# One core, one fused block: a load moved ahead of two others on the sync queue, other warming products at the end, another DRAM layout for the convolution's input

## The chip, the core and the metric

The kernel runs on one core of a Trainium2 chip. The metric is the device time of one execution in microseconds. The core has a matrix engine (PE, with PEld its weight loads), a vector engine (DVE), a scalar engine (ACT), a general engine (POOL), and a sync engine (SP) that issues nearly all transfers. All transfers from SP go through one queue, q1, that 16 DMA engines serve.

## The reference

The input x has 128 samples of 32 channels by 512. Per sample, and with float32 results to match:

```
# 1: a 1x1 convolution whose weights are a softmax mix of 8 sets, chosen per sample by cond
agg_w = einsum('bk,koi->boi', att, weight); y = einsum('boi,bih->boh', agg_w, x) + agg_b
# 2: causal attention on y, 32 query heads, 8 key/value heads, head size 16, rope; residual
x = x + attention(y, Wq, Wk, Wv, Wo)
# 3: a grouped convolution along the 512, 9 taps, 4 groups, plus ctx(cond) and a bias
z = conv_general_dilated(x, weight, padding=[(4, 4)], feature_group_count=4) + ctx + bias
# 4: a linear layer and LoRA experts, weighted by the top 8 of 15 router probabilities; residual
x = x + z @ base_W.T + base_b + lora(z, top8(softmax(z @ router_W.T)))
```

## The kernel before

**Tiling.** The 128 samples are cut into 32 groups of four. A group is a tile of 128 rows (4 samples x 32 channels) by 512 columns. Each large product in reduced float32 (fp32r) is made of three: high by high, high by low, low by high.

**Stages.** Every engine runs a function `steps(t)`, for t from -1 to 33, with the middle in a hardware loop. Step t works on three groups at once: group t+1 gets its mixing and its queries, keys and values (`mix`, `queries`, `keys_values`); group t its scores, softmax, values and output projection (`scores`, `transpose_p`, `values`, `project`); group t-1 its convolution (`conv`); group t-2 the transposition of the convolution's output, the router, the experts and the linear layer (`transpose_z`, `feed_forward`, `transpose_hw`, `lora`). The order within a step is written out by hand, and engines wait for one another by semaphores. `peeled(t, n)` is true where the step is unrolled and t is n; `live(u)` where group u exists.

**The convolution's way.** The nine taps become three products over shifted copies. The sum after attention, `x1`, lies in SBUF with one column of padding on either side (`x1p`, 128 x 4 x 130). SP stores it to a scratch tensor `x1_dram` (L367) and, once that has landed, loads it back three times, shifted by 0, 1 and 2 columns, into 3 x 32 partitions of `xc` (L358); `conv` (L579) waits for the three.

**The sync queue.** SP issues in program order; a wait stops all that is behind it. Before its steps it loads group 0's and 1's x, the values of group 0 (`load_values`: a store of `vS` to DRAM, a wait for it, four loads into `vB`), `baseW` (1 MB), and it stores the mixing weights of groups 4 to 31 (448 KB, L345), waits for that store, and reads them back in their block form in four loads (L277) with pieces of 128 bytes, followed by the 1792 KB broadcast of the mixing biases (`mixb`, L348). These late weights are first used in step 3. Only then comes step 0, whose first issue is group 2's x (`xm`, L354). In a step the order is: x of group t+2, the three loads of `xc` for group t-1, the values of group t+1, the output of group t-2, the store of `x1p` of group t, and `xr`.

**The end.** In step 32 (`G`) no attention is left. PE has the linear layer, router and experts of group 30, then 28 products of 32 rows by 512 columns in bfloat16 whose result nobody reads (`keep_warm`, L433), then the convolution of group 31. Step 33 has the linear layer, router and experts of group 31.

Of the kernel before, what the change touches and what calls it, by code (L numbers as in the profile page):

```python
# [7 lines left out]
F32 = mybir.dt.float32  # L8
# [7 lines left out]
P = 128  # L16
# [53 lines left out]
def live(u):  # L70

    return not isinstance(u, int) or 0 <= u < G
# [13 lines left out]
def build(nc, x, cond, fside, cW0, cb0, cW1, cb1, cW2, cb2, cweight, cbias, Wq, Wk, Wv, Wo,  # L86
          convw, convc, baseW, baseb, routerW, routerb, loraA, loraB, emap, const, out):
    with ExitStack() as ctx:
# [3 lines left out]
        def sem(name):  # L92
            return ctx.enter_context(nc.semaphore(name))
# [102 lines left out]
        oT_lo = sb("oT_lo", [P, NQ, NB, S], F32R)  # L196
        x1p = sb("x1p", [P, PH, P + 2])
        x1 = x1p[:, :, 1:P + 1]
        xc = scratch[0:SHIFTS * S, 0:NB * PH * P].rearrange("p (q n) -> p q n", n=P)
        z_hi = sb("z_hi", [P, PH, P], F32R)  # L200
        z_lo = sb("z_lo", [P, PH, P], F32R)
        arS = sb("arS", [P, NAR])
# [13 lines left out]

        mixb_dram = nc.dram_tensor("mixb_dram", [B, S], F32, kind="Internal").ap()
        v_dram = nc.dram_tensor("v_dram", [P, P], F32, kind="Internal").ap()
        x1_dram = nc.dram_tensor("x1_dram", [NB * PH, CG * PH, P + 2], F32, kind="Internal").ap()
        mixw_dram = nc.dram_tensor("mixw_dram", [B, S, S], F32, kind="Internal").ap()  # L220

        bank = [ctx.enter_context(nc.psum_tensor(f"bank{i}", [P, 512], F32)) for i in range(0)]
# [39 lines left out]
        ar_ps, ar_sb, lg_sb, top_sb = sem("ar_ps"), sem("ar_sb"), sem("lg_sb"), sem("top_sb")  # L262
        ex_sb, top2_sb, rest_sb, sel_sb, selE_sb = sem("ex_sb"), sem("top2_sb"), sem("rest_sb"), sem("sel_sb"), sem("selE_sb")
        we_sb, hw_sb, hwT_ps, hwT_hi_sb, hwT_lo_sb = sem("we_sb"), sem("hw_sb"), sem("hwT_ps"), sem("hwT_hi_sb"), sem("hwT_lo_sb")
        ffn_ps, last_sb, out_sb = sem("ffn_ps"), sem("last_sb"), sem("out_sb")

        x_g = x.rearrange("(g b) s d -> g (b s) d", b=NB)
        out_g = out.rearrange("(g b) s d -> g (b s) d", b=NB)
# [26 lines left out]
        @block.sync  # L295
        def _(sp):

            sp.dma_start(condS[:, :], cond).then_inc(ld["cond"], 16)
            sp.dma_start(cst[:, :], const).then_inc(ld["const"], 16)
            sp.dma_start(cW0S[:, :], cW0).then_inc(ld["cW0"], 16)  # L300
            sp.dma_start(cb0S[:, :], cb0.rearrange("(p a) -> p a", a=1)).then_inc(ld["cb0"], 16)
            sp.dma_start(cbiasS[:, :], cbias).then_inc(ld["cbias"], 16)
            sp.dma_start(cvS[:, :], convw.rearrange("o i k -> o (i k)")).then_inc(ld["convw"], 16)
            sp.dma_start(ccS[:, :], convc).then_inc(ld["cc"], 16)
            sp.dma_start(fsideS[:, :], fside.rearrange("(a o) -> a o", a=1)).then_inc(ld["fside"], 16)
            sp.wait_ge(ld["cW1"], 16)
            sp.wait_ge(ld["cb1"], 16)
            sp.dma_start(xm[:, :], group(x_g, 0)).then_inc(xm_in, 16)
            for c in range(KC):
                sp.dma_start(rawq[:, c, :], Wq[c * P:(c + 1) * P, :]).then_inc(ld[f"wq{c}"], 16)  # L310
            sp.dma_start(rawkv[:, :, 0:P], Wk.rearrange("(c p) n -> p c n", p=P)).then_inc(ld["wkv"], 16)
            sp.dma_start(rawkv[:, :, P:2 * P], Wv.rearrange("(c p) n -> p c n", p=P)).then_inc(ld["wkv"], 16)
            for j in range(PH):
                sp.dma_start(rawB[:, j, :, :], loraB.rearrange("e (p j) r -> j p e r", j=PH)[j]).then_inc(ld["B"], 16)
            sp.dma_start(rawA, loraA.rearrange("e r l -> (e r) l")).then_inc(ld["A"], 16)
            sp.dma_start(rawR[0:NR, :], routerW).then_inc(ld["R"], 16)
            sp.wait_ge(aggb_sb, 1)
            sp.dma_start(mixb_dram, aggb[:, :]).then_inc(aggb_dram, 16)
            for k in range(NKV):
                sp.dma_start(rawo[HD * k:HD * (k + 1), :, :],  # L320
                             Wo.rearrange("(k g d) n -> k d g n", k=NKV, g=NQ)[k]).then_inc(ld["wo"], 16)

            mixb_row = mixb_dram.rearrange("b s -> (b s)")
            sp.wait_ge(y_ps, 1)
            sp.dma_start(xm[:, :], group(x_g, 1)).then_inc(xm_in, 16)
            sp.wait_ge(aggb_dram, 16)
            sp.dma_start(mixb[:, P:4 * P], mixb_row[P:4 * P].partition_broadcast(P)).then_inc(mixb_in, 16)

            def load_values(u):

                sp.wait_ge(vS_sb, u + 1)
                sp.dma_start(v_dram.rearrange("(m b) c -> b m c", b=NB), vS[:, :]).then_inc(v_out, 16)
                sp.wait_ge(v_out, 16 * (u + 1))
                for k in range(HK):
                    sp.dma_start(vB[S * k:S * (k + 1), :, :, HD * k:HD * (k + 1)].rearrange("m b h d -> m (b h) d"),
                                 v_dram.rearrange("(m b) (h k d) -> k m (b h) d", b=NB, h=2, d=HD)[k]).then_inc(vB_in, 16)

            sp.wait_ge(pads_sb, 1)
            load_values(0)
            sp.dma_start(xr[:, :], group(x_g, 0)).then_inc(xr_in, 16)  # L340
            sp.dma_start(rawbase, baseW.rearrange("(p j) l -> p j l", j=PH)).then_inc(ld["base"], 16)
            sp.wait_ge(mixw_zero, 1)
            sp.wait_ge(aggw_act, 1)
            sp.wait_ge(aggw_dve, 1)
            sp.dma_start(mixw_dram[4 * NB:B, :, :], aggS[4 * NB:B, :, :]).then_inc(mixw_out, 16)  # L345
            sp.wait_ge(mixw_out, 16)
            load_mixw(sp, 4, G, mixw_in)
            sp.dma_start(mixb[:, 4 * P:], mixb_row[4 * P:].partition_broadcast(P)).then_inc(mixb_in2, 16)  # L348

            def steps(t):  # L350

                if live(t + 2):
                    sp.wait_ge(y_ps, t + 2)
                    sp.dma_start(xm[:, :], group(x_g, t + 2)).then_inc(xm_in, 16)  # L354
                if live(t - 1):
                    sp.wait_ge(x1_out, 16 * t)
                    for s in range(SHIFTS):
                        sp.dma_start(xc[S * s:S * (s + 1), :, :],  # L358
                                     x1_dram[:, :, s:s + P].rearrange("q r n -> r q n")).then_inc(xc_in, 16)
                if live(t + 1):  # L360
                    load_values(t + 1)
                if live(t - 2):
                    sp.wait_ge(out_sb, t - 1)
                    sp.dma_start(group(out_g, t - 2), outS).then_inc(out_st, 16)
                if live(t):
                    sp.wait_ge(x1_sb, t + 1)
                    sp.dma_start(x1_dram.rearrange("q (i j) n -> (q i) j n", j=PH), x1p[:, :, :]).then_inc(x1_out, 16)  # L367
                if live(t) and live(t + 1):
                    sp.dma_start(xr[:, :], group(x_g, t + 1)).then_inc(xr_in, 16)

            for t in range(0, 4):
                steps(t)
            with sp.Fori(4, G - 2) as t:
                steps(t)
            for t in range(G - 2, G + 2):
                steps(t)
            sp.wait_ge(out_st, 16 * G)

        @block.tensor
        def _(pe):  # L380
# [49 lines left out]
            def keep_warm(products):  # L430

                for _ in range(products):
                    mm(ps[:, 0, :], query16[0:S, :], causal16[0:S, :], start=True, stop=True)  # L433

            def prepare_base(phases):

# [83 lines left out]
            def lora(u):  # L520

                pe.wait_ge(hwT_hi_sb, u + 1)
                pe.wait_ge(hwT_lo_sb, u + 1)
                for n, (a, b) in enumerate(((hwT_hi, lora_hi), (hwT_hi, lora_lo), (hwT_lo, lora_hi))):
                    mm(ps[:, 6, 0:BASE6], a[:, :], b[:, 0:BASE6], start=False, stop=(n == 2))  # L525
                    last = mm(ps[:, 2, 0:P], a[:, :], b[:, BASE6:D], start=(n == 0), stop=(n == 2))  # L526
                last.then_inc(ffn_ps, 1)

            def project(u):

# [90 lines left out]
            def steps(t):  # L621
# [3 lines left out]
                    pe.wait_ge(base_lo_sb, PH)  # L625
                if live(t - 2):
                    transpose_z(t - 2)
                if peeled(t, -1):
                    pe.wait_ge(mixw0_sb, 1)
                    pe.wait_ge(aggb_sb, 1)  # L630
# [28 lines left out]
                    transpose_p(t)  # L659
                if peeled(t, G - 1):  # L660
                    values(t)
                if live(t - 2):
                    transpose_hw(t - 2)
                if live(t) and not peeled(t, G - 1):
                    values(t)
                if peeled(t, G):
                    lora(t - 2)
                    keep_warm(28)
                if live(t - 1):
                    conv(t - 1)  # L670
                if peeled(t, 1):
                    prepare_base((2, 3))

# [213 lines left out]
        def _(dve):  # L887
# [213 lines left out]
            def output(t):  # L1101

                dve.wait_ge(ffn_ps, t - 1)

                wait(dve, out_st, 16 * (t - 2))
                out3 = outS.rearrange("p (n j) -> p j n", j=PH)
                v.tensor_tensor(out3[:, 0:3, :], ps[:, 6, 0:BASE6].rearrange("p (j n) -> p j n", j=3), x1b[:, 0:3, :], ALU.add)
                v.tensor_tensor(out3[:, 3, :], ps[:, 2, 0:P], x1b[:, 3, :], ALU.add).then_inc(out_sb, 1)  # L1108

            def steps(t):  # L1110
# [89 lines left out]
```

## Time and profile before

| | |
|---|---|
| median of 3 runs | 660.11 us (657.11 to 661.21) |
| the profiled execution | 660.98 us |
| its span on the core | 659.1 us |
| mean granted clock of PE | 0.974 of full |
| PE busy | 627.8 us, 95% |
| DVE, ACT, POOL busy | 476.9, 200.2, 224.5 us |
| chain that ended last | PE 88%, DVE 4%, DMA 4% |

The span is what the profiler saw on the core; the time of that execution is 1.9 us longer. The chain is the work that ended last, followed back from the end. Clock 1.00 is 2.4 GHz, 0.50 is 1.2 GHz.

### The profile page before, as it was taken

How to read it: one execution, taken by the hardware profiler on the slowest of the kernel's cores; microseconds unless marked ns; L12 is line 12 of the kernel's file. 1: busy time of each engine (PE TensorE's matmuls, PEld its weight loads, DVE VectorE, ACT ScalarE, POOL GpSimd, SP SyncE). 2: the span in 40 equal slices, each digit the busy share in tenths (PEclk: the TensorE clock that was granted, in tenths of full speed). 3: DMA queues.
4: the chain of work that ended last, by engine and by line, in shares of the span. 5: the costliest groups of instructions: out<-in, count | busy, mean ns of one | idle time of the engine just before them, and what ended most of it. 6: DMA issues, size and time to landing. Idle time of an engine off the chain costs nothing.

```text
span 659.1 us, 13009 instructions
## 1 busy us (share of the span) xinstructions
PE 627.8 (95%) x4375; PEld 512.9 (78%) x4375; DVE 476.9 (72%) x1169; ACT 200.2 (30%) x475; POOL 224.5 (34%) x181
## 2 busy tenths in 40 slices
PE   5967999999999999999999999999999999999785
PEld 3646888888888888888888888888888888887534
DVE  3555787777887777777788777777778777777612
ACT  4332333233333233323233323332323332332200
POOL 6341333323332333332333333333233333332200
PEclk9997999999999999999999999999999999999956
DMA  7675443544545544344444555434444455433410
GB/s 171 119 215 157 105 108 81 113 88 98 118 116 119 120 120 106 100 86 85 107 118 116 120 120 118 104 98 83 85 116 119 116 120 120 119 87 79 100 41 16
DMA packets 121300, 71.20 MB, mean 108 GB/s; under 512 B 48341, under 2 KB 103285, under 8 KB 121032
## 3 DMA queue, kind: packets, MB, share of 16 engines
q1 hardware_dynamic: 119808, 70.53, 45.7%
q10 hardware_dynamic: 1336, 0.24, 0.2%
q0 software_dynamic: 144, 0.28, 0.2%
q8 instruction: 7, 0.11, 0.1%
q14 instruction: 5, 0.04, 0.0%
HBM read 51.49 MB, written 19.53 MB: 108 GB/s over the span
## 4 chain that ended last, share of the span: by engine, by line
PE 88%; DVE 4%; DMA 4%; SPq 1%; ACT 1%; issue 1%; ACTq 0%; DVEq 0%
PE ps L389 32%; PE ps L559 9%; PE ps L553 8%; PE ps L612 6%; PE ps L571 5%; PE ps L579 5%; PE ps L489 4%; PE ps L525 4%; PE ps L600 4%; DMA mixw_dram<-scratch 2%; PE ps L587 2%; PE ps L543 2%; PE ps L433 2%; PE ps L567 2%; DMA xm<-x 1%; PE ps L526 1%
## 5 line engine op out<-in xcount | busy, mean ns | idle before, releaser
L869 POOL TENSOR_TENSOR qk<-network,t 128x640 f32<-128x640 f32 x31 | 48.2, 1555 | 171.1 <-DVE t L1046 171.1
L389 PE MATMUL ps<-wqkv_hi,y_hi 128*128 128x512 f32 (+1 forms) x256 | 87.5, 342 | 1.6 <-DVE raw L1065 1.5
L389 PE MATMUL ps<-wqkv_hi,y_lo 128*128 128x512 f32 (+1 forms) x256 | 87.3, 341 | 0.0
L389 PE MATMUL ps<-wqkv_lo,y_hi 128*128 128x512 f32 (+1 forms) x256 | 87.1, 340 | 0.0
L881 POOL TENSOR_TENSOR raw<-x1p,basebB 128x512 f32<-128x512 f32 x32 | 49.3, 1541 | 81.8 <-DVE x1p L1119 81.8
L1054 DVE TENSOR_TENSOR qk_t<-ps,cst 128x512 f32<-128x512 f32 x32 | 22.1, 692 | 58.5 <-PE ps L541 58.5
L694 ACT ACTIVATE qk_t<-ps 128x512 f32<-128x512 f32 x32 | 19.1, 597 | 141.5 <-PE ps L543 141.5
L694 ACT ACTIVATE raw<-ps 128x256 f32<-128x256 f32 (+1 forms) x96 | 40.2, 453 | 65.8 <-PE ps L600 64.1
L756 ACT ACTIVATE raw<-raw 128x512 f32<-128x512 f32 x64 | 40.4, 632 | 55.3 <-DVE raw L1065 55.3
L853 POOL TENSOR_TENSOR raw<-raw,rz 128x512 f32<-128x512 f32 x32 | 33.6, 1051 | 66.9 <-DVE rz L1075 66.9
L389 PEld LDWEIGHTS ps<-wqkv_hi,y_hi 128*128 128x128 f32 x256 | 48.7, 190 | 9.3 <-DVE raw L1065 1.9
L389 PE MATMUL ps<-wo_hi,oT_hi 128*128 128x512 f32 x128 | 52.6, 411 | 1.5 <-DVE oT_lo L892 1.5
L389 PEld LDWEIGHTS ps<-wqkv_lo,y_hi 128*128 128x128 f32 x256 | 48.7, 190 | 6.0
L389 PEld LDWEIGHTS ps<-wqkv_hi,y_lo 128*128 128x128 f32 x256 | 48.6, 190 | 5.9
L876 POOL TENSOR_TENSOR raw<-raw,zero 128x512 f32<-128x512 f32 x32 | 33.3, 1042 | 54.1 <-DVE raw L1108 54.1
L1063 DVE TENSOR_REDUCE mx<-ps 128x16 f32<-128x512 f32 x64 | 43.9, 686 | 10.7 <-PE ps L571 10.7
L389 PE MATMUL ps<-wo_hi,oT_lo 128*128 128x512 f32 x128 | 50.7, 396 | 0.0
L389 PE MATMUL ps<-wo_lo,oT_hi 128*128 128x512 f32 x128 | 50.5, 395 | 0.0
L861 POOL TENSOR_TENSOR y_lo<-ys,y_hi 128x512 fp32r<-128x512 f32 x31 | 40.0, 1290 | 17.5 <-ACT y_hi L694 17.5
L1065 DVE TENSOR_TENSOR raw<-ps,mx 128x512 f32<-128x512 f32 x64 | 44.3, 692 | 2.2
L559 PE MATMUL ps<-ffn_lo,z_hi 128*128 128x384 f32 x128 | 43.7, 342 | 0.0
L559 PE MATMUL ps<-ffn_hi,z_lo 128*128 128x384 f32 x128 | 43.5, 339 | 0.0
(180 smaller groups left out, 1488.8 us busy)
## 6 DMA issues: line engine op xcount, KB each, us to landing
scratch<-x_dram SPq DMA_DIRECT2D x96, 256.0 KB, 5.0
x_dram<-x1p SPq DMA_DIRECT2D x32, 260.0 KB, 2.2
xm<-x SPq DMA_DIRECT2D x32, 256.0 KB, 3.5
xr<-x SPq DMA_DIRECT2D x32, 256.0 KB, 2.7
out<-raw SPq DMA_DIRECT2D x32, 256.0 KB, 2.1
v_dram<-vS SPq DMA_DIRECT2D x32, 64.0 KB
vB<-v_dram SPq DMA_DIRECT2D x128, 16.0 KB, 2.1
mixb<-mixb_dram SPq DMA_DIRECT2D x1, 1792.0 KB, 8.2
```

What stands on the lines that cost most here:

```text
L389: last = mm(dst, a, b, start=(n == 0), stop=(n == 3 * len(left) - 1))
L553: last = mm(ps[:, 7, 0:P + NAR], a, b[:, BASE6:D + NAR], start=(n == 0), stop=(n == len(terms) - 1))
L559: mm(ps[:, 6, 0:BASE6], a, b[:, 0:BASE6], start=(n == 0), stop=False)
L612: last = mm(ps[P // 2 * h:P // 2 * (h + 1), 4, b * P:(b + 1) * P], vB[:, b, h, :], prT[:, 2 * b + h, :], start=True, stop=True)
L694: return nc.scalar.activation(dst, src, ACT.Copy)
L756: nc.scalar.activation(pr[:, D * h:D * (h + 1)], sx[:, D * h:D * (h + 1)], ACT.Exp, scale=HD ** -0.5).then_inc(p_sb, 1)
L853: nc.gpsimd.tensor_tensor(p3, p3, rz[:, 0:16].unsqueeze(2).broadcast_to([P, 16, S]), ALU.mult).then_inc(pn0_sb, 1)
L861: nc.gpsimd.tensor_tensor(y_lo[:, :], ys[:, :], y_hi[:, :].bitcast(F32), ALU.subtract).then_inc(y_lo_sb, 1)
L869: nc.gpsimd.tensor_tensor(qk[:, :], t1, t2[:, :], ALU.add).then_inc(qk_sb, 1)
L881: nc.gpsimd.tensor_tensor(x1c, x1, basebB[:, :].rearrange("p (n j) -> p j n", j=PH), ALU.add).then_inc(x1c_sb, 1)
L1063: v.tensor_reduce(m, s3, AX.X, ALU.max).then_inc(mx_sb, 1)
L1065: v.tensor_tensor(sx[:, D * h:D * h + D].rearrange("p (h m) -> p h m", m=S), s3, m.unsqueeze(2).broadcast_to([P, 16, S]), ALU.subtract).th ...
```

## The change

Four edits. **Sync queue:** the load of group 2's x now stands ahead of `baseW`; the wait for the mixing weights' store, their four loads and the `mixb` broadcast become a function `late_mixing`, called in step 0 behind group 1's values. **Warming products:** the 28 are gone; instead, full-row fp32r products of 128 x 512 (`wo_hi` by `wo_hi`) stand in runs of three or four: in step 32, four ahead of `transpose_hw`, three behind it, three behind `conv`; in step 33, three behind `transpose_z` and three behind `transpose_hw`. **Experts' product:** in every group the three products for the first 384 columns come first and signal by themselves; the three for the last 128 columns follow and signal `last_ps`, for which DVE's second addition waits. **Layout:** `x1_dram` is stored row by row of the convolution, so that each of the 32 rows is 16 x 130 contiguous numbers; the three loads take one run of 2078 numbers per partition, and `xc` has a row step of 130.

```
-        x1_dram = nc.dram_tensor("x1_dram", [NB * PH, CG * PH, P + 2], F32, kind="Internal").ap()
+        x1_dram = nc.dram_tensor("x1_dram", [CG * PH, NB * PH, P + 2], F32, kind="Internal").ap()
...
+            sp.wait_ge(y_ps, 2)
+            sp.dma_start(xm[:, :], group(x_g, 2)).then_inc(xm_in, 16)
             sp.dma_start(rawbase, baseW.rearrange("(p j) l -> p j l", j=PH)).then_inc(ld["base"], 16)
...
-            sp.wait_ge(mixw_out, 16)
-            load_mixw(sp, 4, G, mixw_in)
-            sp.dma_start(mixb[:, 4 * P:], mixb_row[4 * P:].partition_broadcast(P)).then_inc(mixb_in2, 16)
+
+            def late_mixing():
+
+                sp.wait_ge(mixw_out, 16)
+                load_mixw(sp, 4, G, mixw_in)
+                sp.dma_start(mixb[:, 4 * P:], mixb_row[4 * P:].partition_broadcast(P)).then_inc(mixb_in2, 16)
 
             def steps(t):
 
-                if live(t + 2):
+                if live(t + 2) and not peeled(t, 0):
...
                     for s in range(SHIFTS):
-                        sp.dma_start(xc[S * s:S * (s + 1), :, :],
-                                     x1_dram[:, :, s:s + P].rearrange("q r n -> r q n")).then_inc(xc_in, 16)
+                        sp.dma_start(xcF[S * s:S * (s + 1), 0:x1_row],
+                                     x1_dram.rearrange("r q n -> r (q n)")[:, s:s + x1_row]).then_inc(xc_in, 16)
                 if live(t + 1):
                     load_values(t + 1)
+                if peeled(t, 0):
+                    late_mixing()
...
-                    sp.dma_start(x1_dram.rearrange("q (i j) n -> (q i) j n", j=PH), x1p[:, :, :]).then_inc(x1_out, 16)
+                    sp.dma_start(x1_dram.rearrange("r q n -> q r n"), x1p[:, :, :]).then_inc(x1_out, 16)
...
-                    mm(ps[:, 0, :], query16[0:S, :], causal16[0:S, :], start=True, stop=True)
+                    mm(ps[:, 0, :], wo_hi[:, 0, 0:P], wo_hi[:, 1, :], start=True, stop=True)
...
-                for n, (a, b) in enumerate(((hwT_hi, lora_hi), (hwT_hi, lora_lo), (hwT_lo, lora_hi))):
-                    mm(ps[:, 6, 0:BASE6], a[:, :], b[:, 0:BASE6], start=False, stop=(n == 2))
+                terms = ((hwT_hi, lora_hi), (hwT_hi, lora_lo), (hwT_lo, lora_hi))
+                for n, (a, b) in enumerate(terms):
+                    last = mm(ps[:, 6, 0:BASE6], a[:, :], b[:, 0:BASE6], start=False, stop=(n == 2))
+                last.then_inc(ffn_ps, 1)
+                for n, (a, b) in enumerate(terms):
                     last = mm(ps[:, 2, 0:P], a[:, :], b[:, BASE6:D], start=(n == 0), stop=(n == 2))
-                last.then_inc(ffn_ps, 1)
+                last.then_inc(last_ps, 1)
...
+                if peeled(t, G + 1):
+                    keep_warm(3)
...
+                if peeled(t, G):
+                    pe.wait_ge(sx_sb, 2 * G)
+                    keep_warm(4)
                 if live(t - 2):
                     transpose_hw(t - 2)
...
+                if peeled(t, G) or peeled(t, G + 1):
+                    keep_warm(3)
                 if peeled(t, G):
                     lora(t - 2)
-                    keep_warm(28)
                 if live(t - 1):
                     conv(t - 1)
+                if peeled(t, G):
+                    keep_warm(3)
...
+                dve.wait_ge(last_ps, t - 1)
                 v.tensor_tensor(out3[:, 3, :], ps[:, 2, 0:P], x1b[:, 3, :], ALU.add).then_inc(out_sb, 1)
```

SP's issues from group 0's `xr` on, before; `scratch<-x_dram` are the loads of `xc`, `raw<-L_ffn_base_W` is `baseW`:

```order
L340 DMA xr<-x 128x512
L341 DMA raw<-L_ffn_base_W 128x2048
L345 DMA mixw_dram<-scratch 112x1024
L277 DMA mixw<-mixw_dram 32x28x32 x4
L348 DMA mixb<-mixb_dram 128x3584
L354 DMA xm<-x 128x512
L332 DMA v_dram<-vS 4x32x128
L335 DMA vB<-v_dram 32x8x16 x4
L367 DMA x_dram<-x1p 128x520
L369 DMA xr<-x 128x512
L354 DMA xm<-x 128x512
L358 DMA scratch<-x_dram 32x16x128 x3
```

The same stretch with the change (its line numbers are those of the new file):

```order
L342 DMA xr<-x 128x512
L344 DMA xm<-x 128x512
L345 DMA raw<-L_ffn_base_W 128x2048
L349 DMA mixw_dram<-scratch 112x1024
L334 DMA v_dram<-vS 4x32x128
L337 DMA vB<-v_dram 32x8x16 x4
L278 DMA mixw<-mixw_dram 32x28x32 x4
L355 DMA mixb<-mixb_dram 128x3584
L376 DMA x_dram<-x1p 16x32x130
L378 DMA xr<-x 128x512
L361 DMA xm<-x 128x512
L365 DMA scratch<-x_dram 32x2078 x3
```

Group 2's x and group 1's values moved ahead of the late weights; the store of group 0's `x1p` still stands behind them, now directly.

PE in step 32, from the experts' product of group 30 to the transposition of group 31, before:

```order
L619 MATMUL ps<-cst,hw 128x128
L525 MATMUL ps<-lora_hi,hwT_hi 128x384
L526 MATMUL ps<-lora_hi,hwT_hi 128x128
L525 MATMUL ps<-lora_lo,hwT_hi 128x384
L526 MATMUL ps<-lora_lo,hwT_hi 128x128
L525 MATMUL ps<-lora_hi,hwT_lo 128x384
L526 MATMUL ps<-lora_hi,hwT_lo 128x128
L433 MATMUL ps<-causal,query 128x512 x28
L579 MATMUL ps<-scratch,convW 32x512 x4
L587 MATMUL ps<-cst,raw 128x128 x4
```

With the change:

```order
L442 MATMUL ps<-wo_hi 128x512 x4
L631 MATMUL ps<-cst,hw 128x128
L442 MATMUL ps<-wo_hi 128x512 x3
L535 MATMUL ps<-lora_hi,hwT_hi 128x384
L535 MATMUL ps<-lora_lo,hwT_hi 128x384
L535 MATMUL ps<-lora_hi,hwT_lo 128x384
L538 MATMUL ps<-lora_hi,hwT_hi 128x128
L538 MATMUL ps<-lora_lo,hwT_hi 128x128
L538 MATMUL ps<-lora_hi,hwT_lo 128x128
L591 MATMUL ps<-scratch,convW 32x512 x4
L442 MATMUL ps<-wo_hi 128x512 x3
L599 MATMUL ps<-cst,raw 128x128 x4
```

The 28 between the experts' product and the convolution are gone; runs of three and four stand around the router's transposition (L619, now L631) and behind the convolution.

## Rows read from the trace of the kernel before

**Rows 1.** The page: PE's share of the span; one DMA issue, KB each, us to landing

```profile
PE 627.8 (95%) x4375; PEld 512.9 (78%) x4375; DVE 476.9 (72%) x1169; ACT 200.2 (30%) x475; POOL 224.5 (34%) x181
...
x_dram<-x1p SPq DMA_DIRECT2D x32, 260.0 KB, 2.2
```

**Rows 2.** PE's waits, 80 to 590 us: us in total, times, longest

```profile
PE ps L619 <- DVE hw L1033: 0.4, 1, 0.4
```

**Rows 3.** The chain of waits, 28 to 68 us: start us, us, what

```profile
28.34 2.52 DMA v_dram<-vS
...
45.18 8.09 DMA xm<-x
...
53.31 2.07 PE ps L489 x8
...
66.12 1.00 PE ps L579 x8
```

**Rows 4.** Timeline of SP's issues: start us, us, engine, line, out<-in

```profile
42.27 2.09 SPq L277 DMA_DIRECT2D mixw<-mixw_dram  x4
...
45.65 0.56 SPq L332 DMA_DIRECT2D v_dram<-vS  x1
53.43 2.51 SPq L335 DMA_DIRECT2D vB<-v_dram  x4
```

**Rows 5.** Timeline, 36 to 53 us: the last work ahead of the idle stretch

```profile
41.16 0.27 ACT L694 ACTIVATE vS<-ps 128x128 f32<-128x128 f32 x1
...
45.13 0.60 PE L543 MATMUL ps<-cst,qk 128*128 128x128 f32 x4
...
47.06 1.51 POOL L881 TENSOR_TENSOR raw<-x1p,basebB 128x512 f32<-128x512 f32 x1 [4.88 <-DVE x1p L1119]
```

**Rows 6.** Windows of 1 us: width, busy PE, PEld, DVE, ACT, POOL, clock, DMA, GB/s

```profile
48.00:49.00 1.00, 0.00 (x0) 0.00 (x0) 0.00 (x0) 0.00 (x0) 0.57 (x1) 0.73 1.06 444
...
58.00:59.00 1.00, 1.00 (x7) 1.00 (x8) 0.97 (x2) 0.00 (x0) 0.11 (x1) 0.65 0.52 188
...
627.00:628.00 1.00, 0.33 (x1) 0.14 (x1) 0.27 (x2) 0.28 (x1) 0.00 (x0) 1.00 1.12 199
628.00:629.00 1.00, 0.76 (x5) 0.79 (x5) 0.10 (x1) 0.00 (x0) 0.00 (x0) 0.86 0.19 30
```

**Rows 7.** The chain of waits, 622 to 657 us

```profile
622.13 1.75 PE ps L553 x12
...
628.24 0.41 PE ps L525
...
629.65 12.05 PE ps L433 x28
641.71 1.91 PE ps L579 x8
...
644.39 1.13 PE ps L587 x4
...
647.00 3.06 PE ps L553 x12
...
653.37 0.30 PE ps L619
...
654.44 0.41 PE ps L525
...
655.52 0.84 DVE raw L1107
```

**Rows 8.** Timeline of group 31's loads of `xc`, and the landing of the third (issued 624.26)

```profile
623.37 1.38 SPq L358 DMA_DIRECT2D scratch<-x_dram  x3
...
DMA to landing us min/median/max: 5.1/5.1/5.1
```

**Rows 9.** Timeline of a step in the loop: loads of `xc`, and the convolution

```profile
332.88 1.39 SPq L358 DMA_DIRECT2D scratch<-x_dram  x3
...
342.24 1.06 PE L579 MATMUL ps<-scratch,convW 96*32 96x512 f32 x8
```

More of the change, by code:

```diff
@@ L198, in build @@
         x1 = x1p[:, :, 1:P + 1]
-        xc = scratch[0:SHIFTS * S, 0:NB * PH * P].rearrange("p (q n) -> p q n", n=P)
+        xcF = scratch[0:SHIFTS * S, 0:NB * PH * (P + 2)]
+        xc = xcF.rearrange("p (q n) -> p q n", n=P + 2)[:, :, 0:P]
         z_hi = sb("z_hi", [P, PH, P], F32R)
@@ L264, in build @@
         we_sb, hw_sb, hwT_ps, hwT_hi_sb, hwT_lo_sb = sem("we_sb"), sem("hw_sb"), sem("hwT_ps"), sem("hwT_hi_sb"), sem("hwT_lo_sb")
-        ffn_ps, last_sb, out_sb = sem("ffn_ps"), sem("last_sb"), sem("out_sb")
+        ffn_ps, last_ps, last_sb, out_sb = sem("ffn_ps"), sem("last_ps"), sem("last_sb"), sem("out_sb")
         x_g = x.rearrange("(g b) s d -> g (b s) d", b=NB)
@@ L323, in _ @@
             mixb_row = mixb_dram.rearrange("b s -> (b s)")
+            x1_row = NB * PH * (P + 2) - 2
             sp.wait_ge(y_ps, 1)
```

## The prediction, written before the changed kernel was run

> **What bounds the kernel now.** I read the page first: PE is busy 95% of the span, the next engine 72% [rows 1]. Then PE's waits: in the 510 us between 80 and 590 there is one, of 0.4 us [rows 2]. So the loop is bound by PE's own products, and whatever this change saves lies before 80 or after 590. The chain of waits shows two places. At the start it runs through the landing of group 2's x: issued at 45.18, landed 8.09 us later; PE's last product before it ended at 45.73 (45.13 + 0.60), its next begins at 53.31: 7.6 us of idle PE [rows 3, 5]. At the end, 28 products that nobody reads hold 12.05 us of the chain [rows 7].
>
> The windows add the clock. It falls at 48.5 (0.73 in that slice), 2.7 us after PE went idle, and is back at 58.7 (0.65), 5.4 us after the work resumed; at the end it falls at about 628.7 (0.86), just ahead of the 28 products, which then run at 1.2 GHz and do not bring it back in 12 us [rows 6, 7]. The convolution takes 1.00 us at 2.4 GHz and 1.91 at 1.2 [rows 3, 7].
>
> **The sync queue.** The removed wait is worth 7.6 us and the half clock behind it up to half of 5.4, 2.7 us. From 53.31 to the convolution of group 0 at 66.12 there are 12.8 us; at full clock that stretch is 10.1 at least, and 10.6 if part of it was waiting for DVE. With x there in time it starts at 45.7, so PE is ready for that convolution at 56.3 (55.8 to 56.8), 9.8 us earlier. That is what the edit would give alone.
>
> What is late next is the convolution's input. The store of group 0's `x1p` stood behind the late weights before, and stands directly behind them now; but the late weights themselves start later, since group 1's values come first. Step by step on SP:
> - group 1's `vS` is there at 41.43 [rows 5]. Its store takes 2.5 us to land [rows 3], to 43.95; the 1.4 MB of `baseW` and mixing weights ahead of it, now with 256 KB of x more, may make it 44.4. I take 44.2.
> - the four `vB` loads take 2.5 us to issue [rows 4]: 46.7. The `mixw` loads start there; before it was 42.27 [rows 4], so everything late is 4.4 us later.
> - The queue delivers in order: group 1's values, a store of 64 KB issued at 45.65 right behind the `mixb` broadcast and x, did not land before 53.4, when the loads that wait for it start, 7.8 us instead of 2.5 [rows 4, 3]. Group 2's x, second behind the 2.2 MB, landed at 53.27, 11.0 us after the first `mixw` load [rows 3, 4]. The store of `x1p`, ready since 47.0 (POOL starts on it at 47.06 [rows 5]), now has that place: 46.7 + 11.0 = 57.7, plus the cost of its smaller pieces (below), 58.3.
> - the three loads of `xc`: from the first issue at 623.37 to the third landing at 624.26 + 5.1 = 629.37 are 6.0 us [rows 8]. Old form: 64.3. New form: 62.2 to 64.3; I take 63.4.
>
> So PE stands still from 56.3 to 63.4, 7.1 us, nearly as long as before. The convolution comes 2.7 us earlier than at 66.12, and the clock, which fell 2.7 us into the old gap, falls in this one too; before, it had been back for 7 us when the convolution came, now about 5.4 us of work at 1.2 GHz follow it, 2.7 us lost. **Sum: 0**, between 1.5 us gained and 1.5 lost, if the queue works as the rows show.
>
> **The layout.** The store of `x1p` goes from 128 pieces of 2080 bytes to 512 of 520. No row has such a store. Lower bound: as now, 2.2 us [rows 1]. Upper: the loads of `xc` move 512-byte pieces at 199 GB/s [rows 6], 1.3 us for 260 KB, where the store can't take under nothing: 3.5 us. I take 0.6 us more, nearer the bottom, since most of the 2.2 is not transfer. For the loads, pieces grow from 512 to 8312 bytes. Below: nothing gained. Above: the broadcast, pieces of 14336 bytes, moves 444 GB/s [rows 6], so 768 KB take 1.8 us instead of 3.9, 2.1 us gained. I take 0.9: the broadcast writes 128 partitions, each of these loads 32.
>
> In the loop neither matters: the loads are issued from 332.88 and there 6.0 us later, 338.9, the convolution starts at 342.24 [rows 8, 9]: 3.3 us of slack in each step.
>
> The Trainium skill (SBUF — State Buffer, "Door 1: The DMA port swizzle") speaks against the larger gain: 32 neighbouring partitions reach 8 of the 16 ports that a DMA writes through. With its 435 GB/s for all ports, 218 GB/s for 8 is an estimate of mine, and the loads would then gain 0.3 us whatever the piece: by this rule of the Trainium skill `xc` at the start lands at 64.0, by the broadcast's row at 62.2. The trace's 199 GB/s lies under that ceiling, which doesn't prove it.
>
> On the store, DMA: Bandwidth & Descriptors ("How a descriptor splits into AXI transactions") says that a piece which does not start on a multiple of 256 bytes fetches bytes that it does not use; 520-byte rows start so nearly always. No row shows that cost; it would sit inside the 3.5 us above.
>
> **The experts' product.** The same six products, as many columns and weight loads; the loop gets nothing. DVE's added wait is for products three behind those it waited for, and over before its first addition (0.84 us) is. At the very end DVE now starts after three products instead of six: before 1.08 us after their start (655.52 - 654.44 [rows 7]), now some 0.75, **0.3 gained**.
>
> **The end.** At full clock, step by step, by [rows 7] unless said:
> - the 28 products go: **12.05**.
> - four products ahead of `transpose_hw` lie in the wait for the router; three behind it in the wait for `hwT` (1.07 us from 653.37 to 654.44, less 0.3 for the transposition, against 0.7). One of the 28 takes 12.05 / 28 = 0.43 us at 1.2 GHz, half of it at 2.4; for the heavier type I allow 0.24. Nothing.
> - the experts' product of group 30, 1.41 us (628.24 to 629.65) with the clock falling in it, takes 1.08 as that of group 31: 0.3.
> - PE is ready for the convolution at 629.3. Its input landed at 629.37; 0.6 later for the store, 0.9 earlier for the loads: 0 to 0.7 of waiting, I take 0.2 lost.
> - the convolution 1.91 to 1.00: 0.9. The transpositions, 1.13 to 0.55: 0.6. The router's products, 3.06 to 1.75, as in the step before: 1.3. From there to `transpose_hw` the chain went through DVE and ACT, 3.3 us at either clock: nothing.
> - three products behind the convolution (0.7) fit under DVE's addition of the bias (0.77, from 643.62 to 644.39); three behind the transpositions under 1.5 us of waiting: nothing.
>
> Sum 12.05 + 0.3 + 0.3 - 0.2 + 0.9 + 0.6 + 1.3 = **15.3 us**.
>
> **Against the runs.** 660.98 of the profiled execution less 15.3 is 645.7; that execution is 0.9 above the median, so **644.8** by the runs.
>
> **The rivals.**
> 1. *The start gains too.* If the store of `x1p` overtakes the broadcast, it lands 2.8 us after its issue at some 49.7 (46.7 and 3 us for issuing five loads), and the three loads 5.1 to 6.0 us on, at about 58: a stall of some 1.7 us, too short for the clock to fall. Gain 66.1 - 58 = 8.1 us instead of 0, at most the 9.8 from above. Time 636.7, down to 635.0. Against it speaks the store of `vS`, which overtook nothing [rows 4]. In between lies a broadcast that is done sooner: each us off the stall is one us, and below 2.7 us of stall the clock's 2.7 come on top. Chance 0.15 for the full case, 0.07 for the cases between.
> 2. *The clock falls at the end all the same.* PE still waits for the router ahead of `transpose_hw`, and for the bias and the split of group 31. Then the 0.3, 0.9, 0.6 and 1.3 are not gained, and the three products behind the convolution take 1.3 us at 1.2 GHz, 0.5 beyond their cover: 3.6 us less, gain 11.7: 648.4. For it: the old clock fell without any idle stretch as long as at the start. Against: 13 full-row products, about 3.1 us, are added between the router of group 30 and the linear layer of group 31, and with the products of all rows the clock came back at 58.7, while 32-row ones did nothing for it. Chance 0.16.
> 3. *Slower: the layout breaks the loop.* Store, wait, loads, convolution follow each other in each step, with 3.3 us of slack. Should the store of 520-byte pieces take more than 2.2 + 3.3 = 5.5 us (with the loads as before), each us beyond costs about 30 us in all. To turn 15.3 gained into 6.6 lost it takes 22 us, 0.7 a step, a store of 6.2 us: nearly three times as long. The bound above is 3.5. Chance 0.02, and 0.01 that it eats the gain just to within 1%.
> 4. *The change does not do what it says*: the stall moves from the load to the convolution is my forecast itself for the first edit. That the 28 products were no cost, because `xc` was what PE waited for, is excluded: it landed at 629.4, when they began.
>
> **How the numbers follow.** Forecast (stall moved, clock kept) 0.57; the rivals 0.22, 0.16, 0.03; 0.02 for what I don't see. The forecast's own range is 643 to 646.5, from the 1.5 us of the start on either side. For 8 in 10 it reaches up to the second rival with a lost start, 649.5, and down through the cases between to 637. 1% is 6.6 us, about what a measurement of this kernel tells from no change: faster 0.96, the same 0.02, slower 0.02.
>
> **What the profile after would show.** Right: PE's wait for `xm` gone, one of 5 to 8 us for `scratch<-x_dram` in its place, ending at about 63.4; the clock at 0.50 behind it; `vB` of group 1 issued near 44, the `x1p` store landing near 58; no wait in the loop; clock 1.00 from 620 to the end; the last convolution about 12 us earlier; the end of PE's work about 1 us after the last `hwT`. Wrong: a convolution of group 0 before 60 (rival 1), a low clock after the last projection (rival 2), a wait for `x_dram` in the loop (rival 3).

## The result and the profile after

The changed kernel takes 651.78 us (651.24 to 653.86, 4 runs) against 660.66 (657.11 to 662.28, 4 runs) for the kernel before: a ratio of 0.9879, 95% interval 0.9832 to 0.9925. It is faster by 1.2%, where 2.3% was forecast; 651.8 lies above the range that ended at 649.5. The profiled execution took 651.24 us with a span of 649.3, 9.8 us less than before; 15.3 had been summed.

PE's waits of the changed kernel, whole span: us in total, times, longest.

```profile
PE ps L591 <- DMA scratch<-x_dram: 10.7, 3, 8.0
```

Neither this line nor one like it was among the waits before. The wait for group 2's x is gone, and the convolution (L591, before L579) waits three times for its input: 8.0 us at the start, 1.0 in step 31, 1.8 before the last one. The DMA issues show what has become slower behind the last two of them (for the first, see below); KB each and median us from issue to landing, the first line from before, the two others after:

```profile
scratch<-x_dram SPq DMA_DIRECT2D x96, 256.0 KB, 5.0
...
scratch<-x_dram SPq DMA_DIRECT2D x96, 259.8 KB, 4.3
x_dram<-x1p SPq DMA_DIRECT2D x32, 260.0 KB, 4.5
```

The store of `x1p` takes 4.5 us where it took 2.2 [rows 1]: 4.0 at the least in 32 groups, where it had been 3.7 at the most. One load of `xc` lands 0.7 us sooner in the median.

**The start.** SP's issues (start us, us), and then the chain of waits:

```profile
44.16 2.51 SPq L337 DMA_DIRECT2D vB<-v_dram  x4
46.71 2.42 SPq L278 DMA_DIRECT2D mixw<-mixw_dram  x4
```

```profile
50.00 9.04 DMA x_dram<-x1p
...
59.90 4.99 DMA scratch<-x_dram
...
64.93 1.93 PE ps L591 x8
66.86 1.91 PE ps L451 x8
68.78 3.92 PE ps L398 x12
```

The first late load is issued at 46.71 (forecast 46.7). The store behind the late weights lands at 59.04 (forecast 58.3), its loads at 64.89 (63.4). The first convolution starts 1.2 us earlier than before [rows 3], at 1.2 GHz, and the clock, which fell at 60.9, is back only at 71.1 (the columns are those of [rows 6]):

```profile
60.00:61.00 1.00, 0.00 (x0) 0.00 (x0) 0.00 (x0) 0.00 (x0) 0.00 (x0) 0.93 1.15 316
...
71.00:72.00 1.00, 1.00 (x5) 0.78 (x5) 0.00 (x0) 0.00 (x0) 0.00 (x0) 0.95 0.00 0
```

So the transposition of queries behind the first output projection starts at 72.70 instead of 71.09: the start loses 1.6 us.

**The end.** The chain of waits, from the store of group 30 on (L442 are the warming products, L599 the transpositions of the convolution's output, L565 the router's products, L631 is the transposition in `transpose_hw`):

```profile
607.48 4.43 DMA x_dram<-x1p
...
617.83 1.07 PE ps L591 x8
...
623.88 3.99 DMA x_dram<-x1p
...
628.70 4.88 DMA scratch<-x_dram
...
633.62 1.32 PE ps L591 x8
634.94 1.58 PE ps L442 x3
636.52 0.87 PE ps L599 x4
...
638.87 1.76 PE ps L565 x12
...
643.88 0.33 PE ps L631
...
645.80 0.83 DVE raw L1127
```

The 28 products are gone from it, and the store and the loads stand in their place. The last convolution starts 8.1 us earlier than at 641.71 [rows 7], and right then the clock falls once more, to come back at 637.7:

```profile
634.00:635.00 1.00, 1.00 (x9) 0.14 (x1) 0.01 (x1) 0.00 (x0) 0.00 (x0) 0.65 0.27 102
...
637.00:638.00 1.00, 1.00 (x5) 0.75 (x3) 0.00 (x0) 0.59 (x1) 0.00 (x0) 0.64 0.00 0
```

### The profile page after: what moved, and what is told of

It reads as the page before. It is cut to its first block, busy times and chain, and to the rows that moved or that the text cites. A ratio compares the mean times of both kernels' runs of the same rounds, so it can differ in the third digit from the quotient of the medians.

```text
span 649.3 us, 12985 instructions
## 1 busy us (share of the span) xinstructions
PE 616.8 (95%) x4363; PEld 508.9 (78%) x4363; DVE 474.8 (73%) x1169; ACT 200.3 (31%) x475; POOL 224.6 (35%) x181
## 4 chain that ended last, share of the span: by engine, by line
PE 88%; DMA 6%; DVE 3%; SPq 1%; ACT 1%; issue 1%; DVEq 0%
PE ps L398 34%; PE ps L571 9%; PE ps L565 8%; PE ps L624 6%; PE ps L591 5%; PE ps L583 5%; PE ps L498 4%; PE ps L612 4%; PE ps L535 3%; DMA x_dram<-x1p 3%; DMA scratch<-x_dram 2%; PE ps L599 2%; PE ps L555 2%; PE ps L579 1%; PE ps L538 1%
## 5 line engine op out<-in xcount | busy, mean ns | idle before, releaser
L591 PE MATMUL ps<-scratch,convW 96*32 96x512 f32 x256 | 35.3, 623 | 10.7 <-DMA scratch<-x_dram 10.7
```

What stands on the lines that cost most here:

```text
L591: last = mm(ps[S * g:S * (g + 1), 5, :], convW[:, g, :, :].rearrange("p j o -> p (j o)"), xc.rearrange("p (b g) n -> p g b n", g=S // CG)[ ...
```

## The experiments

Ratios are to the kernel before, with 95% intervals. The start of this kernel varies between executions: the wait for group 2's x, 7.6 us in the profile before, was 2.8, 4.4 and 4.8 us in three others whose start has the old order. Where the end is compared, I therefore count from the end of the last output projection. The end varies too: from there to the end of the span it is 38.9 us in the profile before, 37.8 with the new layout alone and 36.6 with the new order alone, all three with the 28 products. So differences between single profiles of the end carry an uncertainty of some 2 us, unless the waits and the clock in them explain the difference.

### The old layout in the changed kernel

```
-                        sp.dma_start(xcF[S * s:S * (s + 1), 0:x1_row],
-                                     x1_dram.rearrange("r q n -> r (q n)")[:, s:s + x1_row]).then_inc(xc_in, 16)
+                        sp.dma_start(xc[S * s:S * (s + 1), :, :],
+                                     x1_dram[:, :, s:s + P].rearrange("q r n -> r q n")).then_inc(xc_in, 16)
...
-                    sp.dma_start(x1_dram.rearrange("r q n -> q r n"), x1p[:, :, :]).then_inc(x1_out, 16)
+                    sp.dma_start(x1_dram.rearrange("q (i j) n -> (q i) j n", j=PH), x1p[:, :, :]).then_inc(x1_out, 16)
```

Expected: 

> The changed kernel with the old layout of x1_dram and of its three loads; the other three edits stay. Theory (the store in 520-byte pieces lands 1.9 us later, 4.0 to 4.4 us instead of 2.1, and this costs wherever the convolution waits for it): the store lands in about 2.2 us again, the first convolution starts near 63.4 instead of 64.9, the wait of 1.0 us in step 31 is gone, the wait of 1.8 us before the last convolution shrinks to 0.2 or less, and with it the clock stays at 1.00 to the end, which is worth 1.5 us more. Sum 1.5 + 1.0 + 1.6 + 1.5: some 646 us. Rival A (the clock falls at the end whatever the wait): the same without the last 1.5, some 647.7. Rival B (the store is slow for its place in the queue, not for its pieces): 651.8, no change.

Measured: 648.46 us, ratio 0.9827 (0.9788 to 0.9867), which overlaps the changed kernel's interval; the reading rests on the profile. The waits, the DMA issue and the chain of its profile:

```profile
PE ps L589 <- DMA scratch<-x_dram: 6.9, 1, 6.9
```

```profile
x_dram<-x1p SPq DMA_DIRECT2D x32, 260.0 KB, 2.2
```

```profile
66.38 1.94 PE ps L589 x8
...
631.57 1.06 PE ps L589 x8
632.64 0.90 PE ps L440 x3
633.53 0.59 PE ps L597 x4
```

The store takes 2.2 us again, the waits in step 31 and before the last convolution are gone, and with them the fall of the clock at the end: the convolution takes 1.06 us. The span is 3.2 us shorter than the changed kernel's although the first convolution starts 1.5 us later than there (66.38; group 1's values came a microsecond later). By places: 0.8 lost up to the transposition of queries at the start, 1.1 gained from there to the end of the last projection, 2.9 behind it, which is the wait and the clock. Rival B is out: the store was slow for its layout, not for its place. Rival A did not happen in this execution: without the wait the clock stayed. That it was 648.5 and not 646 is the start, which the old layout did not make any faster: the store landed 12.8 us after the first `mixw` load was issued, against 12.3 in the changed kernel, and the three loads took 5.7 us against 5.8.

### The new layout alone

The kernel before with the layout of the change and nothing else.

Expected: 

> The kernel before with the new layout alone. Theory: the store takes 4.0 to 4.5 us in every step, the three loads about 0.3 us less than before; the loop hides it, step 31 pays 1.0 us, the last convolution pays nothing since its input lands under the 28 products: 661 to 662 us. Rival (the layout is harmless and only the queue order shifted the stores): store 2.2 us, 660.7 us, no wait in step 31.

Measured: 660.79 us, ratio 1.0026 (0.9994 to 1.0057). Its DMA issue in the profile:

```profile
x_dram<-x1p SPq DMA_DIRECT2D x32, 260.0 KB, 4.4
```

The wait in step 31 is 0.5 us, another of 1.4 stands at the first convolution, and there is none in the loop or before the last. The 28 products and the loop hid the slow store; the layout shows its price only once the products are gone. It gained nothing either.

### The order on the sync queue alone

The kernel before with the first of the four edits and nothing else.

Expected: 

> The kernel before with the sync queue's order of the change alone. Theory (the stall moves from group 2's x to group 0's convolution, since the store of x1p stands behind the late weights): no wait for xm, a wait of about 7 us for scratch<-x_dram ending near 63.5, the clock low until some 69 us; 659.5 to 661.5 us, no change. Rival (the start gained and other things lost it): the first convolution before 60 us and 651 to 653 us.

Measured: 662.39 us, ratio 1.0034 (1.0011 to 1.0057): slower by 0.3%. PE's waits:

```profile
PE ps L586 <- DMA scratch<-x_dram: 9.2, 1, 9.2
```

The convolution of group 0 starts at 66.17 and runs for 1.94 us. The wait for x has become a wait for the convolution's input. The convolution starts as late as before (66.12), and now the work at 1.2 GHz follows it: the transposition of queries starts at 72.69 instead of 71.09. The rival, a start that gained, is out.

This profile also shows the 28 products from another side. They start at full clock, and the clock falls under them while PE is busy without a gap; the chain, and two windows:

```profile
630.90 10.16 PE ps L440 x28
```

```profile
632.00:633.00 1.00, 1.00 (x6) 0.40 (x5) 0.00 (x1) 0.00 (x0) 0.92 (x1) 0.91 0.11 43
633.00:634.00 1.00, 1.00 (x3) 0.29 (x2) 0.00 (x0) 0.00 (x0) 0.12 (x1) 0.50 0.58 219
```

### The late weights behind group 0's convolution input

In `late_weights_later` the layout is the old one, and the late weights are moved once more (against the changed kernel, without the lines of the layout):

```
                 if live(t - 1):
                     sp.wait_ge(x1_out, 16 * t)
+                    if peeled(t, 1):
+                        sp.wait_ge(mixw_out, 16)
                     for s in range(SHIFTS):
...
+                if peeled(t, 1):
+                    late_mixing()
                 if live(t + 1):
                     load_values(t + 1)
-                if peeled(t, 0):
-                    late_mixing()
```

Expected: 

> Old layout, and the late weights moved once more: in step 1, behind group 0's three loads of xc and ahead of group 2's values. Theory: the store of x1p is issued at 46.7 and lands at 49, xc near 55, the first convolution starts at 56.4 without a wait and the clock never falls: 9 to 10 us less than the run with the old layout, some 636.5 us. Rival (the late weights take the next transfer instead: values or x1p of group 1 are late in step 2): a wait of 2 to 5 us on vB or scratch<-x_dram between 65 and 85 us, 639 to 642 us.

Measured: 639.43 us (639.12 to 640.11), ratio 0.9686 (0.9648 to 0.9725). The timelines of PE and then SP:

```profile
58.86 1.06 PE L591 MATMUL ps<-scratch,convW 96*32 96x512 f32 x8
```

```profile
49.10 0.33 SPq L376 DMA_DIRECT2D x_dram<-x1p  x1
...
51.14 1.52 SPq L365 DMA_DIRECT2D scratch<-x_dram  x3
52.71 6.01 SPq L277 DMA_DIRECT2D mixw<-mixw_dram  x4
```

The store is issued and landed within 2 us, and the first convolution starts without a wait, 7.5 us earlier than in the run with the old layout and at full clock. PE's waits have one more, of 1.0 us, for the convolution's input in step 2: the rival's wait, but smaller than its 2 to 5 us. It is 9.0 us less than in `old_layout`, where 9 to 10 were expected; the time itself lies 2.9 above the expected 636.5 and in the rival's range, since `old_layout` had come out at 648.5 and since here too group 1's values came late, so that the store was issued at 49.1 and not at 46.7. This is the fastest kernel of the study by its ratio.

### The same pair with the new layout

Expected: 

> The late weights in step 1 as in late_weights_later, with the new layout of x1_dram. The pair differs by the layout alone. Theory: the store lands in 4.0 to 4.5 us instead of 2.2; a wait of about 1 us in step 31, one of 1 to 2 us before the last convolution, 0 to 1 us before the first: 642 to 643.5 us against 639.4. Rival (the longer store is hidden once the queue is free): 639.4, as the pair's other kernel.

Measured: 646.5 us (643.2 to 649.37), ratio 0.9800 (0.9763 to 0.9836), against 0.9686 with the old layout. PE's waits in its profile, 40 to 80, 80 to 590 and from 590 us:

```profile
PE ps L593 <- DMA scratch<-x_dram: 2.2, 1, 2.2
...
PE ps L593 <- DMA scratch<-x_dram: 0.7, 1, 0.7
...
PE ps L593 <- DMA scratch<-x_dram: 2.3, 2, 1.6
```

Its span is 3.9 us longer than the old layout's (641.3 against 637.4), and the waits are the theory's: 2.2 us of the difference lie ahead of the end of the last projection, 1.7 behind it. The intervals of the two ratios do not overlap, so here the price of the layout shows in the times as well. At the end PE waits 1.6 us for the last convolution's input and the clock stays at 1.00; at the start it falls, at 59.0, and the first convolution takes 1.93 us. The profiled execution was the fastest of four that spread over 6 us; what the other three lost on top, no trace shows.

### What makes the store slow

Rows of 192 or of 144 numbers in `x1_dram`, same store, loads in pieces of 512 bytes:

```
-        x1_dram = nc.dram_tensor("x1_dram", [CG * PH, NB * PH, P + 2], F32, kind="Internal").ap()
+        x1_dram = nc.dram_tensor("x1_dram", [CG * PH, NB * PH, 192], F32, kind="Internal").ap()
...
+                    sp.dma_start(x1_dram[:, :, 0:P + 2].rearrange("r q n -> q r n"), x1p[:, :, :]).then_inc(x1_out, 16)
```

Expected, 768 bytes: 

> The changed kernel with rows of 192 numbers (768 bytes) in x1_dram: the store still moves 512 pieces of 520 bytes, now each from a multiple of 256 bytes; the three loads take pieces of 512 bytes. If the pieces' starts (and that neighbours share a line of DRAM) make the store slow, it lands in 2.2 to 2.8 us; if their number does, in 4.0 to 4.5 us as in the changed kernel. Only the store's time is read from this run; the loads should take about what they did before the change, 5.0 us.

Expected, 576 bytes: 

> The same with rows of 144 numbers (576 bytes): pieces start on multiples of 64 bytes, mostly not of 256. If only a shared line of 64 bytes is slow, the store lands in 2.2 to 2.8 us; if the start has to be a multiple of 256 bytes, it stays above 3 us where pitch768's is below; if the number of pieces is the cause, 4.0 to 4.5 us like pitch768.

Measured, the DMA issues of the two, in this order:

```profile
x_dram<-x1p SPq DMA_DIRECT2D x32, 260.0 KB, 3.4
```

```profile
x_dram<-x1p SPq DMA_DIRECT2D x32, 260.0 KB, 3.6
```

Neither theory alone. Of the 2.3 us between 2.2 and 4.5, pieces that start on a grid and no longer adjoin each other give 0.9 (576) to 1.1 (768) back. Most of it comes back already with starts on multiples of 64 bytes, of which one in four is a multiple of 256; whether the starts or the gaps between the pieces do it, these two runs can't tell. 1.2 us remain with 512 pieces in place of 128, each on its own row. Whether their number or their order in DRAM costs that was not told apart. The times, one run each (648.48 and 655.28), aren't compared.

The two say something of the clock as well. In both PE waits 1.8 us for the last convolution's input, as in the changed kernel. The chains of 768 and then of 576:

```profile
632.09 1.07 PE ps L591 x8
```

```profile
636.66 1.93 PE ps L591 x8
```

At 768 the clock stays at 1.00 to the end of PE's work; at 576 it falls at 636.6. So the same wait doesn't always bring the fall.

### No 28 products, and 28 of all rows

In the kernel before, the call of 28 products is taken out (`no_28`), or its product replaced (`full_row_28`):

```
-                    mm(ps[:, 0, :], query16[0:S, :], causal16[0:S, :], start=True, stop=True)
+                    mm(ps[:, 0, :], wo_hi[:, 0, 0:P], wo_hi[:, 1, :], start=True, stop=True)
```

Expected, none: 

> The kernel before without the 28 warming products and with nothing in their place. Theory (all of their 12 us lay on the path, since xc had landed): 12 us less, less up to 0.5 for xc, 648.5 to 649.5 us, with the clock low over the last convolution. Rival (part of their time covered the load of xc or the output of group 30): 651 to 654 us.

Measured: 647.56 us, ratio 0.9796 (0.9767 to 0.9825). Its chain:

```profile
622.70 5.21 DMA scratch<-x_dram
627.95 1.98 PE ps L579 x8
```

From the last projection to the end of the span 26.8 us remain of 38.9: 12.1 us, all of the products' time in the profile before. Against the two other profiles with the 28 products it is 11.0 and 9.8 us; there the products took 11.35 and 10.16 us, since the clock fell 0.7 and 1.9 us behind their start and not 0.9 ahead of it. This removal alone is faster than the whole change (its interval lies just below that of 0.9832 to 0.9925). The time of 647.56 lies 1 us below the 648.5 to 649.5 that were expected.

Expected, all rows: 

> The kernel before, its 28 warming products replaced by 28 full-row ones of 128 x 512 in reduced float32, at the same place. Theory (products of 32 rows do not bring the clock back, full-row ones do): the clock is back 3 to 7 us after the 28 begin, they take some 9 us instead of 12, and the last convolution runs at 2.4 GHz: about 3 + 0.9 + 0.6 + 1.3 = 6 us less than before, some 654.5 us. Rival (rows make no difference): 12 us of products, clock 0.50 until 652, about 660.5 us.

Measured: 654.17 us, ratio 0.9892 (0.9871 to 0.9913). Chain and window:

```profile
627.86 7.37 PE ps L433 x28
635.23 1.04 PE ps L579 x8
```

```profile
629.00:630.00 1.00, 1.00 (x4) 0.81 (x3) 0.00 (x0) 0.00 (x0) 0.94 (x1) 0.66 0.12 47
```

The clock is back at 629.7, 1.8 us after the products begin, sooner than the expected 3 to 7; in 12 us of 32-row products it did not come back [rows 7], nor in the two other profiles that have them. So the kind of the products decides. That it is the rows, as the theory said, isn't shown: the full-row products are reduced float32 where the 32-row ones are bfloat16, and no run changes one without the other. From the last projection to the end of the span 32.5 us remain of 38.9, 6.4 less (expected 6), and 7.4 us are still products that nobody needs. The clock did not stay either: it falls again at 639.9, in the router's products, which take 2.47 us.

### No warming products in the fastest kernel

Expected: 

> late_weights_later without any warming product. Theory (the short full-row products keep the clock at 2.4 GHz over the end): without them it falls between the last projection and the end, the last convolution takes up to 1.9 us instead of 1.0, the transpositions 1.1 instead of 0.6, the router's products up to 3.0 instead of 1.8: 641 to 643 us. Rival (nothing but the 28 products was the cost, and the clock would have stayed): 639.0 to 639.4, clock 1.00 throughout.

Measured: 641.83 us (638.03 to 642.17), ratio 0.9698 (0.9662 to 0.9734); the interval overlaps that of the kernel with them, so the times don't decide. In the profile the clock falls at 628.3; the window, and then the chain:

```profile
628.00:629.00 1.00, 0.88 (x5) 0.91 (x6) 0.00 (x0) 0.00 (x0) 0.00 (x0) 0.67 0.00 0
```

```profile
624.15 1.04 PE ps L591 x8
...
628.12 2.89 PE ps L565 x12
```

From the last projection to the end of the span it is 24.6 us, against 23.5 with the products, whose router products take 1.77: the 16 products are worth 1.1 us in these two executions. Another of the four executions without them took 638.03 us at a mean clock of 0.997, less than any with them (639.12 at least). No trace shows its end; its mean clock suggests that the fall does not come in every execution. What the products are worth on the average stays open.

## Why the prediction was wrong

**The step that failed** is the term of the layout, "I take 0.6 us more, nearer the bottom, since most of the 2.2 is not transfer". The store takes 2.3 us more in the median, 1.9 at the end (2.06 to 3.99), beyond the upper bound of 1.3. The bound was taken from loads of 512-byte pieces; that their rate also holds for stores of such pieces was not in any row, and neither was it that most of the 2.2 is not transfer. For the loads I took 0.9 of gain. At the end, where it counted, they gained 0.3: 5.7 us from the first issue to the last landing against 6.0. (Over all 32 groups the median of that stretch falls from 6.5 us to some 5.7, but in the loop nobody waits for it.) Behind this term hang three others:

- *Step 31.* The 3.3 us of slack were worked out for the loop, and with the end's 6.0 us for the loads; in the step of [rows 9] itself the third load lands 6.6 us after the first issue, which leaves 2.7. That was still enough. Step 31 has no next group's queries and less slack; I did not look there. It pays 1.0 us.
- *Before the last convolution* I allowed 0.2 us of waiting. From the last projection's end to that convolution the change saves 10.7 us instead of 12.15, so 1.5 are lost, with a wait of 1.8 us.
- *The clock.* It fell at 634.3, just behind that wait. From the last convolution's start to the start of `z_hi` 3.8 us pass before and after, and 1.5 should have gone. This was the second rival (0.16) in part, by a cause that I did not name there: its 0.9 and 0.6 were not gained, its 0.3 and 1.3 were. In the run with the old layout there was no wait and no fall; but with a wait of 1.8 us the clock stayed up in `pitch768`, and with one of 1.6 in `late_new_layout`. The wait gives the clock an occasion to fall; that it took it in the profiled execution is in part chance, and no run shows how often it does.

**The start** came at -1.6 us, just outside the 1.5 that I gave on either side of 0. That the stall moves from the load to the convolution held, with its steps: values first, delivery in order, the clock. The order's run says the same with a ratio of 1.0034. The convolution came 1.5 us later than the forecast's 63.4, half from the store's landing and half from the loads (5.8 us against 5.1). That isn't the price of the new layout: with the old one the store landed 12.8 and 11.8 us behind the first `mixw` load (`old_layout`, `order_only`), with the new one 12.3, and the loads took as long with either. What was too short is the 11.0 us for the queue, and the gain for the loads did not come. PE was ready 0.6 us later than forecast (56.9), and its stall lasted 8.0 us, not 7.1.

**What held at the end**: the 28 products were worth 12.1 us, counted against the profile before; the router's products and the chain behind them 1.36 us (1.3); the reordered experts' product 0.2 at the very end (0.3) and nothing in the loop, where from step 1's transposition to step 31's 532.9 us pass after and 533.0 before.

By places, the spans' 9.8 us (5.5 fewer than the 15.3 of the forecast, which are the start's 1.6, step 31's 1.0, and 1.5 on either side of the last convolution's start): the start -1.6, step 31 -1.0, up to the last convolution +10.7, the convolution and transpositions 0, the router's products +1.4, the output +0.2, the tail 0.1.

The rule of the Trainium skill that I weighed (SBUF — State Buffer, "Door 1: The DMA port swizzle") would have given the loads 0.3 us by my estimate. At the end they gained that, but at the start nothing (5.8 us, against 5.7 in `old_layout`) and in the median of the 32 groups some 0.8, so the trace doesn't confirm it. The estimate was also too strict: it put all three loads on the same 8 ports, and by that section's table partitions 64 to 95, where the third goes, lie on the other 8.

The Trainium skill's other rule (DMA: Bandwidth & Descriptors, "How a descriptor splits into AXI transactions") speaks of 256-byte starts and of bytes that are fetched, and I applied it to the starts of pieces that are written. With every start on a multiple of 256 bytes 1.1 us come back, with one start in four 0.9 (`pitch768`, `pitch576`), so these runs leave some 0.2 us for it.

## What to carry to other kernels

When a load is moved ahead on an in-order queue, list what still stands behind the bulk, and when each of those is needed: here the next in line waited nearly as long, and one more move gave 9 us. Slack has to be read in every unrolled step, not in the loop alone, and a cover that is removed (28 idle products) uncovers whatever else was changed under it. A layout that makes loads contiguous can break up the store; measure both sides.

## What the hardware showed beside

- 260 KB stored to DRAM: 2.2 us in 128 pieces of 2080 bytes, 3.4 in 512 of 520 bytes at a pitch of 768, 3.6 at 576, 4.5 at 520.
- Three loads into 32 partitions each gained 0.3 of 6.0 us from pieces 16 times as long in the last group, and some 0.8 of 6.5 in the median of 32 groups.
- 28 products of 32 rows in bfloat16 left the clock at 1.2 GHz for 12 us, and in another execution it fell 1.9 us after they had begun, with PE busy throughout; with 28 products of all rows in reduced float32, at the same place, the clock was back 1.8 us in.
- With a wait of 1.8 us ahead of the last convolution the clock fell in two profiled executions (`after`, `pitch576`) and stayed up in one (`pitch768`).
